# Row sums of two head pairs in four column tiles, the spreading of reciprocals beside the shift, and a new table of feed-forward slots

## What is computed

```python
x = x + 0.5 * ffn(layernorm(x, 1e-5))
x = x + attention(layernorm(x, 1e-5))
x = x + 0.5 * ffn(layernorm(x, 1e-5))

attention(x):  q, k, v = x @ w_q, x @ w_k, x @ w_v       # 16 heads of 64
               o = softmax(q @ k.T / 8) @ v              # per head, 512 x 512
               y = o @ w_proj + b_proj + x
               return layernorm(y, 1e-6) * gamma + beta

ffn(x):        gate, up = fp4(x) @ fp4(w_gate).T, fp4(x) @ fp4(w_up).T   # 352 wide
               return fp4(silu(gate) * up) @ fp4(w_down).T
```

## Time and profile before

| | |
|---|---|
| time, median of 3 runs | 2317.58 us (2314.41 to 2319.59) |
| profiled execution: time, span | 2317.27 us, 2315.5 us |
| mean granted TensorE clock | 0.981 |
| PE busy | 2205.7 us, 95% |
| DVE busy | 1675.1 us, 72% |
| POOL busy | 1468.5 us, 63% |
| ACT busy | 1194.5 us, 52% |

### The profile page before, as it was taken

How to read it: one execution, slowest core, us unless ns; L and a number is a source line. 1 busy time by engine, 2 the same in 40 slices (tenths; PEclk the granted TensorE clock), 3 DMA queues, 4 the chain that set the end, 5 groups by cost and what they waited for, 6 DMA issues and landing times.

```text
span 2315.5 us, 38775 instructions
## 1 busy us (share of the span) xinstructions
PE 2205.7 (95%) x14537; PEld 1120.1 (48%) x14537; DVE 1675.1 (72%) x2736; ACT 1194.5 (52%) x1813; POOL 1468.5 (63%) x1417
## 2 busy tenths in 40 slices
PE   3999999999999999999999999999999999999984
PEld 2344445545454544545455454554545454454542
DVE  5565778777777877777787777877777787776653
ACT  2454555545555555555555455554555555555541
POOL 3365767667566675766667566766756667576652
PEclk8899999999999999999999999999999999999996
DMA  1000000000000000000000000000000000000000
GB/s 58 1 7 2 7 2 6 7 2 11 2 11 2 6 7 2 11 2 7 6 2 11 2 11 2 7 7 2 11 2 11 2 6 7 2 7 2 7 2 10
DMA packets 167496, 15.86 MB, mean 7 GB/s; under 512 B 148304, under 2 KB 166928, under 8 KB 167312
## 3 DMA queue, kind: packets, MB, share of 16 engines
q1 hardware_dynamic: 167312, 13.39, 5.0%
HBM read 7.03 MB, written 4.19 MB: 5 GB/s over the span
## 4 chain that ended last, share of the span: by engine, by line
PE 82%; DVE 12%; issue 4%; POOL 1%; ACT 1%; DMA 0%; SPq 0%; POOLq 0%
PE pS L945 22%; PE pO L972 18%; PE pM L929 9%; PE pX L957 6%; PE pX L993 5%; PE pM L1094 5%; DVE nmax L790 4%; PE pM L982 3%; PE LpF L293 2%; PE FpF L293 2%; PE LpF L269 2%; PE FpF L256 2%; PE LpF L256 1%; DVE ON L891 1%; PE FpF L269 1%
## 5 line engine op out<-in xcount | busy, mean ns | idle before, releaser
L649 POOL TENSOR_TENSOR ES<-ES,E 128x512 f32<-128x512 f32 x512 | 701.2, 1390 | 213.4 <-ACT E L738 210.9
L738 ACT ACTIVATE E<-pS 128x1024 f32<-128x1024 f32 x512 | 523.0, 1021 | 410.6 <-PE pS L945 408.6
L790 DVE TENSOR_REDUCE nmax<-pX 128x2 fp32r<-128x1024 f32 x512 | 622.2, 1215 | 125.6 <-PE pX L957 123.4
L972 PE MATMUL pO<-E,VA 128*64 128x512 f32 x2048 | 552.3, 618 | 0.0
L643 POOL TENSOR_TENSOR ES<-E 128x512 f32<-128x512 f32 x256 | 321.3, 1277 | 258.3 <-ACT E L738 258.1
L929 PE MATMUL pM<-xf,w_raw 128*64 128x512 f32 x1024 | 267.0, 600 | 2.9 <-DVE QL L900 2.2
L957 PE MATMUL pX<-KH,QH 64*128 64x512 f32 x1024 | 249.6, 426 | 8.3 <-DVE nmax L790 5.5
L945 PE MATMUL pS<-QH,KH 64*128 64x512 f32 x1024 | 255.3, 495 | 0.0
L945 PEld LDWEIGHTS pS<-QH,KH 64*128 64x128 f32 x1024 | 95.3, 183 | 253.5 <-issue 252.2
L957 PEld LDWEIGHTS pX<-KH,QH 64*128 64x128 f32 x1024 | 189.8, 306 | 53.0 <-DVE nmax L790 14.9
L945 PE MATMUL pS<-SH,onesr 64*128 64x512 f32 x1024 | 203.2, 393 | 0.0
(11 more groups left out here) (179 smaller groups left out, 3284.5 us busy)
## 6 DMA issues: line engine op xcount, KB each, us to landing
RROW<-RC SPq DMA_DIRECT2D x512, 2.0 KB, 2.0
xin<-in_L_attn_x SPq DMA_DIRECT2D x16, 256.0 KB, 3.0
SH<-nmax SPq DMA_DIRECT2D x256, 2.0 KB, 2.0
LC<-LROW SPq DMA_DIRECT2D x256, 2.0 KB, 2.1
out<-X SPq DMA_DIRECT2D x16, 256.0 KB, 2.5
w_raw<-in_L_attn_w_q SPq DMA_DIRECT2D x1, 512.0 KB, 4.4
w_raw<-in_L_attn_w_k SPq DMA_DIRECT2D x1, 512.0 KB, 5.2
w_raw<-in_L_attn_w_v SPq DMA_DIRECT2D x1, 512.0 KB, 6.1
```

Source lines behind the costliest of these rows:

```text
L649: ins = g.tensor_tensor(ES[par][:, hd, :], ES[par][:, hd, :], E[s][:, hd, :], ALU.add)
L738: a.activation(E[s][:, :, :], pS[:, :, :], ACT.Exp).then_inc(s_exp, 1)
L790: v.tensor_reduce(nmax[px % 2][:, :, t:t + 1], pX[:, :, :], AX.X, ALU.max, negate=True).then_inc(s_max, 1)
L972: ins = pe_.matmul(pO[half(hd), :], VA[of][:, kt, j * 128 + 64 * hd:j * 128 + 64 * hd + 64], E[kt][:, hd, :], start=kt == 0, stop=kt == KT ...
```

## The change

Row sums are taken for two pairs at once, in every second pair (p even), by four matmuls with 32 columns of ones each, into four column tiles of pM; ES gets a third buffer. They stand after the feed-forward pieces of s = 2. LROW, LC, REC, RC and RROW follow in that rhythm: four LC transfers in even pairs, one reciprocal and eight RROW transfers in odd pairs. Spreading, ON, `project` and Yacc come one pair later than before (i - 3 and i - 4).

At s = 3 the shift uses rows 0 to 31 and 64 to 95 in place of 64 rows for each head, and the spreading, with RROW and `sel` moved to partitions 32 to 63, is a third row tile of 32 right behind it. The shift of the other three quarters stays as it is.

The slots of the feed-forward pieces come from two tables now, and several have other values. A slot of the table is counted from a batch's own start, so slot % 32 is the quarter t. X2 has two buffers and X1 three, the output transfer moves to p = 6.

```diff
+class FirstLayer:
+    lead = 1
+    mom_x, scale_x, apply_x = -10, -8, -6
+    max_x, divide_x, magic_x, round_x, rescale_x, turn_x = -5, -4, -4, -3, -2, -1
+    gate, up = (0, 1, 2, 3), (4, 5, 6, 8)
+    max_h, divide_h, magic_h, round_h, rescale_h = (6, 10), (7, 11), (7, 11), (8, 12), (9, 13)
+    turn_h, down, add = (10, 12, 14, 15), 16, 17
+    mom, scale, apply, turn_xm, xf, y0, beta = 18, 19, 20, 21, 22, 22, 32
+class LastLayer:
+    lead = -1
+    mom, scale, apply, gamma = 14, 16, 17, 18
+    mom_x, scale_x, apply_x = 19, 20, 22
+    max_x, divide_x, magic_x, round_x, rescale_x, turn_x = 24, 25, 25, 26, 27, 28
+    gate, up = (29, 30, 31, 32), (33, 34, 38, 40)
+    max_h, divide_h, magic_h, round_h, rescale_h = (36, 43), (40, 44), (42, 46), (47, 48), (48, 49)
+    turn_h, down, add = (49, 50, 51, 52), 54, 55
...
 # SyncE
-                    if there(i - 2, NP):
-                        sp.wait_ge(s_rlo, i - 1)
-                        for hl in range(2):
-                            for hd in range(2):
-                                sp.dma_start(RROW[2 * hl + hd:2 * hl + hd + 1, :].bitcast(F32),
-                                             RC[old][:, hl, hd, :].bitcast(F32)).then_inc(s_rrow, 16)
+                    if p % 2 == 1 and there(i - 2, NP):
+                        sp.wait_ge(s_rlo, i // 2)
+                        for j in range(4):
+                            for hl in range(2):
+                                r = 32 + 4 * hl + j
+                                sp.dma_start(RROW[r:r + 1, :].bitcast(F32), RC[:, hl, j, :].bitcast(F32)).then_inc(s_rrow, 16)
...
-                    if there(i - 1, NP):
-                        sp.wait_ge(s_lrow, i)
-                        for hd in range(2):
-                            sp.dma_start(LC[new][:, hd, :], LROW[64 * hd:64 * hd + 1, :]).then_inc(s_lc, 16)
+                    if p % 2 == 0 and there(i - 1, NP):
+                        sp.wait_ge(s_lrow, i // 2)
+                        for j in range(4):
+                            sp.dma_start(LC[:, j, :], LROW[32 * j:32 * j + 1, :]).then_inc(s_lc, 16)
...
 # VectorE
-                        if s == 3 and there(i - 2, NP):
-                            dve.wait_ge(s_rb, i - 1)
-                            wait(dve, s_proj, i - 2)
-                            v.tensor_tensor(ON[:, :], OT[(p - 2) % 4][:, :], pM[:, :], ALU.mult).then_inc(s_norm, 1)
+                        if s == 3 and there(i - 3, NP):
+                            dve.wait_ge(s_rb, i - 2)
+                            wait(dve, s_proj, i - 3)
+                            v.tensor_tensor(ON[:, :], OT[(p - 3) % 4][:, :], pM[:, :], ALU.mult).then_inc(s_norm, 1)
...
 # TensorE
-                            lhs = kk[half(hd), :] if n == 3 else kk[half(hd), cols]
-                            ins = pe_.matmul(pS[:, hd, :], lhs, qq[half(hd), :], start=n == 0, stop=n == 3)
+                            rows = slice(64 * hd, 64 * hd + 32) if n == 3 and kt == 3 else half(hd)
+                            lhs = kk[rows, :] if n == 3 else kk[rows, cols]
+                            ins = pe_.matmul(pS[:, hd, :], lhs, qq[rows, :], start=n == 0, stop=n == 3)
...
-                def row_sums(i, par):
-                    pe.wait_ge(s_add, 3 * i + 3)
-                    wait(pe, s_norm, i - 1)
-                    pe.wait_ge(s_klo, min(i + 4, NP))
-                    for hd in range(2):
-                        ins = pe_.matmul(pM[half(hd), :], ones[:, 0:64], ES[par][:, hd, :], start=True, stop=True)
+                def row_sums(i):
+                    pe.wait_ge(s_add, 3 * i)
+                    wait(pe, s_norm, min(i - 3, NP))
+                    pe.wait_ge(s_klo, min(i + 3, NP))
+                    for j in range(2):
+                        for hd in range(2):
+                            r = 32 * (2 * j + hd)
+                            ins = pe_.matmul(pM[r:r + 32, :], ones[:, 0:32], ES[(i - 2 + j) % 3][:, hd, :], start=True, stop=True)
                     ins.then_inc(s_l, 1)
...
-                        if s == 3 and there(i - 2, NP):
-                            pe.wait_ge(s_rrow, 64 * (i - 1))
-                            pe.wait_ge(s_lrow, min(i, NP))
-                            wait(pe, s_norm, i - 2)
-                            pe_.matmul(pM[:, :], sel[0:64, :], RROW[0:64, :], start=True, stop=True).then_inc(s_rb, 1)
+                        if s == 3 and there(i - 3, NP):
+                            pe.wait_ge(s_rrow, 128 * ((i - 1) // 2))
+                            pe.wait_ge(s_lrow, min(i, NP) // 2)
+                            pe.wait_ge(s_klo, min(i + 3, NP))
+                            wait(pe, s_norm, i - 3)
+                            pe_.matmul(pM[:, :], sel[32:64, (i - 3) % 2, :], RROW[32:64, :], start=True, stop=True).then_inc(s_rb, 1)
```

More of the change, by code:

```diff
@@ L384, in steps @@
     def steps(eng, body):
-        for b in range(-1, B + 2):
+        for b in range(-2, B + 2):
             for p in range(PAIRS):
@@ L429, in make_program @@
         E = [m.sb(f"E{kt}", [128, 2, S]) for kt in range(KT)]
-        ES = [m.sb(f"ES{i}", [128, 2, S]) for i in range(2)]
+        ES = [m.sb(f"ES{i}", [128, 2, S]) for i in range(3)]
         OT = [m.sb(f"OT{i}", [128, S]) for i in range(4)]
@@ L433, in make_program @@
         LROW = m.sb("LROW", [128, S])
[L434 to L436 removed]
+        LC = m.sb("LC", [128, 4, 4])
+        REC = m.sb("REC", [128, 4, 4])
+        RC = m.sb("RC", [128, 2, 4, 4], F32R)
         RROW = m.sb("RROW", [128, S], F32R)
@@ new lines, in first_ffn @@
+                def first_ffn(b, t):
+                    for c, k in parts_at(FirstLayer, FirstLayer.divide_h, b, t):
+                        F.pool_divide_h(pool, c, k)
+                    for c, k in parts_at(FirstLayer, FirstLayer.rescale_h, b, t):
+                        F.pool_rescale_h(pool, c, k)
+                    for c in batch_at(FirstLayer, FirstLayer.scale, b, t):
+                        norm_x1.scales(nc, pool, neg_half, c)
+                    for c in batch_at(FirstLayer, FirstLayer.y0, b, t):
+                        pool.wait_ge(norm_x1.s_out, c + 1)
+                        wait(pool, norm_y.s_out, c - 1)
+                        g.tensor_tensor(tiles(Yacc[c % 2][:, :]), tiles(F.xm[:, :]), each_tile(bproj),
+                                        ALU.add).then_inc(s_y0, 1)
+                    for c in batch_at(FirstLayer, FirstLayer.beta, b, t):
+                        g.tensor_tensor(tiles(X1[c % 3][:, :]), tiles(X1[c % 3][:, :]), each_tile(beta),
+                                        ALU.add).then_inc(s_x1b, 1)
+                    for c in batch_at(FirstLayer, FirstLayer.scale_x, b, t):
+                        if c > 0:
@@ new lines, in last_ffn_psum, with first_ffn @@
+                def last_ffn_psum(b, t):
+                    for c in batch_at(LastLayer, LastLayer.turn_x + 1, b, t):
+                        L.act_x(act, c)
+                    for c, k in parts_behind(LastLayer, LastLayer.gate, b, t):
+                        L.act_tanh(act, c, k)
+                    for c, k in parts_behind(LastLayer, LastLayer.turn_h, b, t):
+                        L.act_h(act, c, k)
+                def first_ffn(b, t):
+                    for c, k in parts_at(FirstLayer, FirstLayer.magic_h, b, t):
+                        F.act_magic_h(act, c, k)
+                    for c in batch_at(FirstLayer, FirstLayer.apply, b, t):
+                        wait(act, s_y0, c)
+                        norm_x1.apply(nc, act, c, F.xm, X1[c % 3])
+                    for c in batch_at(FirstLayer, FirstLayer.apply_x, b, t):
+                        if c > 0:
@@ new lines, in last_ffn_psum @@
+                def last_ffn_psum(b, t):
+                    for c, k in parts_behind(LastLayer, LastLayer.gate, b, t):
+                        L.dve_silu(dve, c, k)
+                    for c, k in parts_behind(LastLayer, LastLayer.up, b, t):
+                        L.dve_h(dve, c, k)
+                    for c in batch_at(LastLayer, LastLayer.add, b, t):
+                        dve.wait_ge(L.s_down, c + 1)
+                        v.tensor_tensor(X2[c % 2][:, :], L.pF[:, :], X2[c % 2][:, :], ALU.add).then_inc(s_res, 1)
@@ new lines, in first_ffn @@
+                def first_ffn(b, t):
+                    for c, k in parts_at(FirstLayer, FirstLayer.max_h, b, t):
+                        F.dve_max_h(dve, c, k)
+                    for c, k in parts_at(FirstLayer, FirstLayer.round_h, b, t):
+                        F.dve_round_h(dve, c, k)
+                    for c in batch_at(FirstLayer, FirstLayer.mom, b, t):
+                        dve.wait_ge(s_x1, c + 1)
+                        norm_x1.moments(nc, dve, c, X1[c % 3])
+                    for c in batch_at(FirstLayer, FirstLayer.mom_x, b, t):
+                        if c > 0:
@@ new lines, in last_ffn @@
+                def last_ffn(b, t):
+                    for c in batch_at(LastLayer, LastLayer.turn_x, b, t):
```

(10 more changed lines are left out.)

439 lines of the change are left out of this document (160 added, 279 removed).

## The result

The changed kernel takes 2325.66 us (median of 7, 2321.39 to 2328.77) against 2316.32 for the kernel before (2314.04 to 2319.64): a ratio of 1.0041, interval 1.0028 to 1.0053. It is slower by 9 us where I forecast it 12 us faster. The range, 2242 to 2338 us, is so wide that it held the time; the direction was wrong.

What follows compares the result with a forecast made beforehand. Bound: the order of PE instructions, added up from start to start. Sum: -47 + 38 - 20 + 26 - 7 - 3 + 2 - 1 = -12 us, so 2306 us; range 2242 to 2338.

Steps and rivals of the forecast that it cites:

- Row sums (-47): Row sums of two pairs in four column tiles side by side: 1.72 becomes 0.99 us, 64 times, 47 us less.
- The rival of serial row sums: At the row sums: four column tiles run in pairs, not all side by side; +55 us, 2361 us, chance 0.06.
- Part 2 (+38): At s = 3, spread beside the 32-row shift: saves 0.23, shape changes cost 0.53 us; 0.30 x 126 = +38 us.
- the waits at s = 3 (-20): At s = 3, PE's waits for VectorE fall from 1.8 to about 0.5 us per batch: -20 us.
- the 20 and 14 of its part 3: Feed-forward pieces at s = 3: 20 us less waiting, or 14 if the change to 32 rows is free.
- `project` at s = 1 (+26): At t = 5, 9, 13, 25 `project` waits for maxima behind moved VectorE pieces: 3.0 against 1.25 us a batch, +26 us.
- the rival with VectorE further behind: At `project`, t = 5, 9, 13, 25: VectorE pieces slowed by GpSimd's additions; +31 us, 2337 us, chance 0.14.
- The middle (-13): The stretch from the first scores to the tail, 2160.7 us before: counted to change by -13 us.
- the terms of -7 and -3: PE's wait for Yacc at t = 18 goes, -7 us; transposes stand between 128x64 groups in fewer quarters, -3 us.
- Queues and lag: RROW and LC transfers and normalisation one pair later: all covered, nothing counted; uncovered, each 0.5 us at 64 places is 32.
- Ends (+1): Tail +2 us, between -5 (moments of y earlier) and +8 (norm chain); start-up -1, one normalisation less before first Q copy.
- The +8 for the norm chain: In the tail, batch 14's two roundings, turns and down matmuls now stand inside the last norm chain: +8 us.

Runs made afterwards that it cites:

- the first experiment: The changed kernel with the shift and the spread back at 64 rows, everything else as changed: 2304.95 us, 0.9943 of the kernel before.

## Why the prediction failed, step by step

**Row sums (-47): right.** PE in t = 26 into 27 of the changed kernel, answering to the earlier trace rows:

```profile
1135.14 1.06 PE L974 MATMUL pM<-ES,ones 128*32 128x512 f32 x8
1136.14 0.50 PE L935 MATMUL pS<-QH,KH 64*128 64x512 f32 x2
```

1.00 for two pairs, where 0.99 was counted against 1.72: 46 us. The groups of PE by shape have the 512 matmuls at 605 ns each and a busy union of 68.2 us instead of 131.6, so all four column tiles run side by side. The rival of serial row sums falls. (The 1.27 us at which the prediction lets the change lose doesn't follow from its sum: 12 us over 64 groups allow 0.86 + 0.19 = 1.05. And its "V to a transpose", 0.96, is in the earlier trace rows the k matmuls to a transpose; the figure stands.)

**Part 2 (+38) and the waits at s = 3 (-20): the price right, the sum of both nearly so.** 0.32, 0.44 and 0.56 stand where 0.33, 0.44 and 0.55 were written. But the 0.30 reaches the end only where PE doesn't wait: taking part 2 out of the changed kernel gives about 22 us (17.4 in a trace with three stretches at half clock), adding it to the one before costs 15.7, not 38. The prediction let part 2 take the place of 6 us of waits (the 20 and 14 of its part 3); the first experiment shows 0.9 a batch, some 14 us. Since the waits at s = 3 were counted to shrink by 20 in all, the two terms together, +18, were about right, and the +38 alone was not what the part costs. The waits left at s = 3 are 0.35 at t = 27 and little else, in sum as forecast; but pO to the next was to be 0.91 at t = 27, and is 1.26, since V waits there for ON.

**`project` at s = 1 (+26): right in the sum.** 2.65 us a batch at t = 5, 9, 13 and 25 for 3.0; singly 0.31, 0.95, 0.70 and 0.69, where t = 5 was forecast at 0.8. VectorE's rounding takes 0.9 + 0.8 there, not the longer form of the earlier trace rows, so the rival with VectorE further behind falls too.

**The middle (-13): -8.0.** A batch is 137.10 for 136.9. One wait of 0.25 at t = 30, from pO to the gate, was not in the sum: 4 us. And the batch of 137.61 from which the forecast started is the longer of two kinds: three of the twelve inner batches of the kernel before take 137.0, 2 us in all. The rest of the difference and the terms of -7 and -3 I can't separate.

**Queues and lag: right in the middle, wrong in the tail.** No wait on RROW or LC shows in the batches; all the 8.6 us that PE idles for RROW lie in the tail.

**Ends (+1): the step that failed.** It measured +14. For the tail the prediction has -5 for the moments of y, 25 us after the last scores quarter for 30.2, and +8 for the norm chain. The moments start at 32.6, so they came 2.4 later and not 5 earlier: the row sums start 3.2 later than before (10.9 for 7.7), the way from there to the spread is 1.2 longer (13.0 for 11.8), and from the spread to the moments it is 2.0 shorter (8.7 for 10.7). The claim behind the -5, that batch 14's feed-forward chain no longer stands ahead of them, was false: its last two gate and first two up pieces do, each with a trip through VectorE. The +8 for the norm chain was right (+7.3). That the moments came 5 us earlier was meant to pay for it, and this never happened. In the start-up (-1) I followed only the removed normalisation and not the order in which VectorE goes through the two halves of one h (1.2 to 1.5), nor what stands between V and the first scores (+1.6); it measured +4.4, of which 3.5 to 3.8 are the new order.

So the forecast's sign hung on 12 us of gain, and the step that was walked through most briefly was out by 13. "It is wrong if the tail moves over 8 us" is the line of the prediction that came true. That the time lies in the range is luck: the range reaches to 2338 for the sake of rivals about `project` and the row sums, neither of which came true, and it was the ends that brought the time there. The error was also in the chances: none of the rivals was about the ends.

## What to carry to other kernels

Cost a change of tile shape for rows as for columns, in and out, with the weight load it exposes: here packing one more small matmul beside a neighbour saved 0.23 and cost 0.53, since the neighbour had to change its shape for it. When a table of slots is made anew, walk through its first and its last batch as chains of their own, since there every piece lies on the path that the steady state hides. A saving on the bounding engine counts only at those places where that engine doesn't wait next. And before two traces are subtracted, lay their granted clocks side by side.

## What the runs showed that I had not expected

The start-up of one execution moves by some us with nothing changed. In seven kernels whose instructions up to there are the same, the first transposes of h start at 33.4 to 36.4 us and the first scores at 78.3 to 82.0. The first goes with the rise of the granted clock from 0.5 to 1.0 (1.2 to 2.4 GHz), at 21 us in two of them and at 27 in five. And in the first, second and last batch, where PE stands still for part of the time, the clock falls for 3.4 us in some traces, and in the traces of the changed kernel and the one before it doesn't, though PE is busy for only 1.62 of the 3.40 us from 298.00 in the changed kernel's. So I read the start-up by its segments and at equal clock.

Taking the strided weights of pX costs 0.23 once exposed, while `onesr` with 128 columns costs 0.10: of the 0.53 for 32 rows in one quarter, 0.33 is not the change of shape but the two loads that it uncovers. That the stride is what makes the load of pX dearer is my reading; no run takes it away. And a group of three row tiles with 32 rows takes no longer than one of two (0.44 to the next in the changed kernel, 0.43 with two in the run that has 32 rows everywhere).
